# A token-shift expert kernel: the first term of its mix on ScalarE, a second load queue and zero matmuls at the start

## The reference

```python
# x: (8, 1024, 512); 16 experts; w_key (16, 512, 1024); w_value (16, 1024, 512); C = 512 slots per expert
xprev = jnp.concatenate([shift_state[:, None, :], x[:, :-1]], axis=1)
dxprev = xprev - x
xk = x + dxprev * time_maa_k
xr = x + dxprev * time_maa_r
e_idx = token_ids.reshape(N).astype(jnp.int32) * HASH_PRIME % E
...
pos = jnp.take_along_axis(jnp.cumsum(onehot, axis=0), e_idx[:, None], axis=1)[:, 0] - 1
keep = pos < C
...
h = jnp.square(jax.nn.relu(jnp.einsum('ecd,edf->ecf', expert_in, w_key)))
expert_out = jnp.einsum('ecf,efd->ecd', h, w_value)
...
r = jax.nn.sigmoid(jnp.einsum('btd,ed->bte', xr, w_recept))
return r * y            # and x + r * y is the output
```

## Time and profile before

| what | value |
|---|---|
| median of 3 runs | 894.66 us (894.54 to 895.29) |
| span of the profiled execution | 892.5 us |
| TensorE busy | 878.1 us, 98% of the span |
| vector engine busy | 774.1 us, 87% |
| ScalarE busy | 379.8 us, 43% |
| GpSimd busy | 546.4 us, 61% |
| DMA | 186.40 MB, mean 209 GB/s |

### The profile page before, as it was taken

One profiled execution on the slowest core, in us unless ns is written; L12 is line 12 of the kernel. 1 busy time (PEld: TensorE's weight loads), 2 busy tenths in 40 slices (PEclk: granted clock), 3 DMA queues, 4 the chain that ended last, 5 costly groups with the idle time before them and its releaser, 6 DMA issues.

```text
span 892.5 us, 10891 instructions
## 1 busy us (share of the span) xinstructions
PE 878.1 (98%) x3915; PEld 726.6 (81%) x3915; DVE 774.1 (87%) x1060; ACT 379.8 (43%) x582; POOL 546.4 (61%) x485
## 2 busy tenths in 40 slices
PE   6999999999999999999999999999999999999997
PEld 5878888888888888888888888888888888888886
DVE  7999999869898989898989898989898989889862
ACT  4444434555353434443444434343435353535350
POOL 2322215767776767777676777676767677762411
PEclk9999999999999999999999999999999999999999
DMA  9655548865757575858584848484857575754521
GB/s 329 217 176 194 196 142 275 274 218 195 255 176 264 171 270 167 276 169 266 163 278 147 281 147 292 143 286 154 275 167 260 178 253 181 249 192 174 173 87 47
DMA packets 73765, 186.40 MB, mean 209 GB/s; under 512 B 11760, under 2 KB 11760, under 8 KB 73712
## 3 DMA queue, kind: packets, MB, share of 16 engines
q1 hardware_dynamic: 46064, 101.80, 34.9%
q0 software_dynamic: 27648, 83.91, 27.2%
HBM read 152.11 MB, written 33.55 MB: 208 GB/s over the span
## 4 chain that ended last, share of the span: by engine, by line
PE 95%; DVE 2%; issue 1%; DMA 0%; POOL 0%; ACT 0%; SPq 0%; DVEq 0%; POOLq 0%
PE acc L774 32%; PE acc L776 31%; PE acc L775 31%; DVE xr_lo L652 1%; DMA wr_raw<-w_recept_t 0%; DVE mix L643 0%; PE rt_bank L809 0%; DVE mix L646 0%; DVE cum L532 0%; POOL out L359 0%; DVE onehot L526 0%; DVE id_low L524 0%; PE rt_bank L818 0%; DVE totals L536 0%; DVE gate L698 0%
## 5 line engine op out<-in xcount | busy, mean ns | idle before, releaser
L774 PE MATMUL acc<-xk_hi,wk_hi 128*128 128x512 f32 x512 | 199.7, 390 | 0.0
L776 PE MATMUL acc<-xk_hi,wk_lo 128*128 128x512 f32 x512 | 199.6, 390 | 0.0
L775 PE MATMUL acc<-wv_lo,h_hi 128*128 128x512 f32 x512 | 199.5, 390 | 0.0
L774 PE MATMUL acc<-wv_hi,h_hi 128*128 128x512 f32 x512 | 199.5, 390 | 0.0
L776 PE MATMUL acc<-wv_hi,h_lo 128*128 128x512 f32 x512 | 199.4, 390 | 0.0
L775 PE MATMUL acc<-xk_lo,wk_hi 128*128 128x512 f32 x512 | 199.3, 389 | 0.0
L441 ACT ACTIVATE hid<-acc 128x512 f32<-128x512 f32 x128 | 76.6, 599 | 266.1 <-PE acc L776 266.1
L352 POOL DMA_INDIRECT pair_even<-pairs,row_pair x128 | 141.0, 1102 | 65.7 <-issue 38.7
L352 POOL DMA_INDIRECT pair_odd<-pairs,row_pair x128 | 139.7, 1091 | 39.0 <-issue 39.0
L359 POOL DMA_INDIRECT out<-xrow,row_tok x64 | 85.0, 1327 | 111.9 <-DVE xrow L701 102.1
L686 DVE TENSOR_TENSOR hid<-hid 128x512 f32<-128x512 f32 x128 | 88.4, 690 | 51.6 <-ACT hid L441 49.8
(11 more groups left out here) (105 smaller groups left out, 1231.7 us busy)
## 6 DMA issues: line engine op xcount, KB each, us to landing
raw<-w_key SPq DMA_DIRECT2D x64, 512.0 KB, 4.8
raw<-w_value SPq DMA_DIRECT2D x64, 512.0 KB, 4.0
xT<-xs_t SPq DMA_DIRECT2D x64, 256.5 KB, 4.0
gates<-gate SPq DMA_DIRECT2D x64, 256.0 KB, 2.9
pair_even<-pairs,row_pair POOLq DMA_INDIRECT x128, 3.0
pair_odd<-pairs,row_pair POOLq DMA_INDIRECT x128, 3.0
wr_raw<-w_recept_t SPq DMA_DIRECT2D x4, 256.0 KB, 4.6
xrow<-x,row_tok POOLq DMA_INDIRECT x64, 4.8
```

The lines of the kernel that those rows point to most:

```text
L774: pe.matmul(bank[:, :], hi, m_hi, start=first, stop=False)
L775: pe.matmul(bank[:, :], hi, m_lo, start=False, stop=False)
L776: return pe.matmul(bank[:, :], lo, m_hi, start=False, stop=last)
```

## The change

- Loads: `maar` and the first `wr_raw` chunk, as two column halves with a semaphore each, are issued by ScalarE ahead of everything else it does. SyncE loads the first `xT` chunk in two halves, then for k = 1 to 3 `wr_raw` before `xT`. The three first raw weight loads move to the begin of SyncE's step g = 3.
- Mix: the formula becomes x * (1 - maar) + previous * maar. GpSimd makes `keep_r` = 1 - maar. ScalarE writes x * keep_r to the mix slot (`term`), the vector engine adds previous * maar with one instruction (`mix_xr`). The subtractions on the vector engine and on GpSimd are gone, and with them `POOL_DIFF`. The left half of step 0 is mixed in the old way by `mix_left`, which writes `xr_hi` itself.
- Order: ScalarE does term(n + 1) ahead of split_xr(n), and the sigmoids of group g after split 4g + 7 (5 for group 0, 10 for group 1). The vector engine mixes one step ahead of its `xr_lo`.
- TensorE: seven matmuls on zeros into `rt_bank` at the start; steps 0 to 2 run pass by pass, all hi x hi first, each pass with its own wait; step 0 in halves.

```diff
--- before.py
+++ after.py
@@ -74,7 +74,9 @@
...
-    POOL_DIFF = [g * KD + k for g in range(2, 11) for k in (1, 3)]
+    HALF = C // 2
+    WARM = 7
+    SIG_AFTER = [g * KD + min(5 + g, 2 * KD - 1) for g in range(G)]
...
@@ -250,9 +260,14 @@
                 if g >= X_SLOTS:
                     sp.wait_ge(s_mix, KD * (g - X_SLOTS) + k + 1)
                 first = g * C + g // GB
-                sp.dma_start(xT[:, g % X_SLOTS, k, :],
-                             xs_t[k * P:(k + 1) * P, first:first + 1 + C]).then_inc(
-                                 s_x[g % X_SLOTS][k], 16)
+                rows = slice(k * P, (k + 1) * P)
+                if g == 0 and k == 0:
+                    sp.dma_start(xT[:, 0, 0, 0:1 + HALF], xs_t[rows, 0:1 + HALF]).then_inc(s_x_left, 16)
+                    sp.dma_start(xT[:, 0, 0, 1 + HALF:1 + C], xs_t[rows, 1 + HALF:1 + C]).then_inc(
+                        s_x[0][0], 16)
+                else:
+                    sp.dma_start(xT[:, g % X_SLOTS, k, :],
+                                 xs_t[rows, first:first + 1 + C]).then_inc(s_x[g % X_SLOTS][k], 16)
             def store_gates(g):
                 for t in range(ST):
...
-            for k in range(KD):
+            load_group(0, 0)
+            for k in range(1, KD):
+                sp.dma_start(wr_raw[:, k, :], w_recept_t[k * P:(k + 1) * P, :]).then_inc(s_wrec[k], 16)
                 load_group(0, k)
-                if k == 0:
-                    sp.dma_start(maar[:, :], maa_r[:, :]).then_inc(s_maar, 16)
-                sp.dma_start(wr_raw[:, k, :], w_recept_t[k * P:(k + 1) * P, :]).then_inc(s_wrec[k], 16)
             for k in range(KD):
                 load_group(1, k)
             sp.dma_start(id_i, ids.rearrange("b (q j) -> (b q) j", j=J)).then_inc(s_ids, 16)
             sp.dma_start(maak[:, :], maa_k[:, :]).then_inc(s_maak, 16)
-            for n in range(RAW_SLOTS):
-                load_weight(n)
             for k in range(KD):
                 load_group(2, k)
             for g in range(G):
+                if g == 3:
+                    for n in range(RAW_SLOTS):
+                        load_weight(n)
                 if g + X_SLOTS < G:
...
@@ -307,6 +322,8 @@
             pool.affine_select(out=ident[:, :], in_=ident[:, :], compare_op=ALU.not_equal, fill=1.0,
                                base=0, pattern=[[-1, P]], channel_multiplier=1).then_inc(s_ident, 1)
             pool.iota(residue[:, :], [[unhash, E]], base=0, channel_multiplier=0).then_inc(s_table, 1)
+            pool.wait_ge(s_maar, 16)
+            pool.tensor_scalar(keep_r[:, :], maar[:, :], -1.0, 1.0, ALU.mult, ALU.add).then_inc(s_keep, 1)
             pool.memset(segment[:, :, :], 1.0).then_inc(s_zero, 1)
             pool.wait_ge(s_zero, 2)
...
@@ -403,12 +411,25 @@
         @block.scalar
         def _(act):
-            def split_xr(g, k):
-                n = g * KD + k
+            def term(n):
+                g, k = divmod(n, KD)
+                first = HALF if n == 0 else 0
+                act.wait_ge(s_x[g % X_SLOTS][k], 16 * (g // X_SLOTS + 1))
+                if n == 0:
+                    act.wait_ge(s_keep, 1)
+                if n >= MIX_SLOTS:
+                    act.wait_ge(s_rlo, n - MIX_SLOTS + 1)
+                act.activation(mix[:, n % MIX_SLOTS, first:C], xT[:, g % X_SLOTS, k, 1 + first:1 + C],
+                               ACT.Copy, scale=keep_r[:, k:k + 1]).then_inc(s_term, 1)
+            def split_xr(n):
+                g, k = divmod(n, KD)
+                first = HALF if n == 0 else 0
                 act.wait_ge(s_mix, n + 1)
                 if g >= 2:
                     act.wait_ge(s_R, ST * (g - 1))
-                act.copy(xr_hi[:, g % 2, k, :], mix[:, n % MIX_SLOTS, :]).then_inc(s_rhi, 1)
+                act.copy(xr_hi[:, g % 2, k, first:C], mix[:, n % MIX_SLOTS, first:C]).then_inc(s_rhi, 1)
             def sigmoids(g):
                 for t in range(ST):
@@ -444,31 +465,45 @@
                 act.wait_ge(s_sq, n + 1)
                 act.copy(h_hi[:, n % KF, :], hid[:, n % H_SLOTS, :]).then_inc(s_hhi, 1)
-            def split_w_recept(k):
+            def split_w_recept(k, cols=slice(0, D)):
+                act.copy(wr_hi[:, k, cols], wr_raw[:, k, cols]).then_inc(s_wrhi, 1)
+            left, right = slice(0, D // 2), slice(D // 2, D)
+            act.dma_start(maar[:, :], maa_r[:, :]).then_inc(s_maar, 16)
+            act.dma_start(wr_raw[:, 0, left], w_recept_t[0:P, left]).then_inc(s_wrec[0], 16)
+            act.dma_start(wr_raw[:, 0, right], w_recept_t[0:P, right]).then_inc(s_wrec_right, 16)
+            act.wait_ge(s_zeros, 1)
+            act.activation(sigmoid_table[:, :], zeros[:, 0:1], ACT.Sigmoid)
+            act.wait_ge(s_wrec[0], 16)
+            split_w_recept(0, left)
+            act.wait_ge(s_wrec_right, 16)
+            split_w_recept(0, right)
+            term(0)
+            term(1)
+            split_xr(0)
+            for k in range(1, KD):
                 act.wait_ge(s_wrec[k], 16)
-                act.copy(wr_hi[:, k, :], wr_raw[:, k, :]).then_inc(s_wrhi, 1)
...
-            act.activation(sigmoid_table[:, :], ident[:, 0:1], ACT.Sigmoid)
-            for k in range(KD):
                 split_w_recept(k)
-                split_xr(0, k)
...
-            for g in range(G):
-                for k in range(KD):
-                    if g + 1 < G:
-                        split_xr(g + 1, k)
-                    if g * KD + k in FIRST_KEY:
-                        split_weight(FIRST_KEY.index(g * KD + k))
...
-                    if k == min(g, KD - 1):
-                        sigmoids(g)
+                term(k + 1)
+                split_xr(k)
+            for n in range(KD, (G + 1) * KD):
+                r = n - KD
+                if n + 1 < G * KD:
+                    term(n + 1)
+                if n < G * KD:
+                    split_xr(n)
...
+                if n in SIG_AFTER:
+                    sigmoids(SIG_AFTER.index(n))
...
@@ -629,28 +664,38 @@
                                   quarter[:, 0:1], ALU.mult, ALU.add).then_inc(s_rows, 1)
...
-            def mix_xr(g, k):
-                n = g * KD + k
...
-                if n in POOL_DIFF:
-                    dve.wait_ge(s_pool_diff, pool_diffs)
-                else:
-                    if n >= MIX_SLOTS:
-                        dve.wait_ge(s_rlo, n - MIX_SLOTS + 1)
-                    dve.tensor_tensor(slot, xT[:, g % X_SLOTS, k, 0:C], here,
-                                      ALU.subtract).then_inc(s_diff, 1)
-                    dve.wait_ge(s_diff, n + 1 - pool_diffs)
-                dve.scalar_tensor_tensor(slot, slot, maar[:, k:k + 1], here,
-                                         ALU.mult, ALU.add).then_inc(s_mix, 1)
+            def mix_left():
+                slot = mix[:, 0, 0:HALF]
+                before, here = xT[:, 0, 0, 0:HALF], xT[:, 0, 0, 1:1 + HALF]
+                factor = maar[:, 0:1]
+                dve.wait_ge(s_x_left, 16)
+                dve.tensor_tensor(slot, before, here, ALU.subtract).then_inc(s_left, 1)
+                dve.wait_ge(s_left, 1)
+                dve.wait_ge(s_maar, 16)
+                dve.scalar_tensor_tensor(xr_hi[:, 0, 0, 0:HALF], slot, factor, here,
+                                         ALU.mult, ALU.add).then_inc(s_hi_left, 1)
+                dve.scalar_tensor_tensor(slot, slot, factor, here, ALU.mult, ALU.add).then_inc(s_left, 1)
...
+                dve.tensor_tensor(xr_lo[:, 0, 0, 0:HALF], slot, xr_hi[:, 0, 0, 0:HALF].bitcast(F32),
+                                  ALU.subtract).then_inc(s_lo_left, 1)
...
+            def mix_xr(n):
+                g, k = divmod(n, KD)
+                first = HALF if n == 0 else 0
+                slot = mix[:, n % MIX_SLOTS, first:C]
+                dve.wait_ge(s_term, n + 1)
+                dve.scalar_tensor_tensor(slot, xT[:, g % X_SLOTS, k, first:C], maar[:, k:k + 1],
+                                         slot, ALU.mult, ALU.add).then_inc(s_mix, 1)
...
@@ -702,17 +747,18 @@
             route = routing()
-            dve.wait_ge(s_maar, 16)
+            dve.memset(zeros[:, :], 0.0).then_inc(s_zeros, 1)
+            mix_left()
             mixed = 0
             for r in range(-KD, G * KD):
                 n = r + KD
-                while mixed < min(G * KD, n + (1 if n == 0 else min(KD, 2 + max(0, r) // KD))):
-                    mix_xr(*divmod(mixed, KD))
+                while mixed < min(G * KD, n + 2):
+                    mix_xr(mixed)
                     mixed += 1
                 if r < 0:
-                    dve.wait_ge(s_wrhi, n + 1)
+                    dve.wait_ge(s_wrhi, n + 2)
...
@@ -775,6 +821,43 @@
                 pe.matmul(bank[:, :], hi, m_lo, start=False, stop=False)
...
+            def warm():
+                pe.wait_ge(s_zeros, 1)
+                for i in range(WARM):
```

(82 more changed lines are left out.)

15 lines of the change are left out of this document (7 added, 8 removed).

## The result

The changed kernel takes 891.94 us (median of 6 runs, 891.27 to 893.05), the kernel before 894.79 us beside it (6 runs, 894.37 to 895.72): a ratio of 0.9965 with a 95% interval of 0.9955 to 0.9975, 2.85 us less. The forecast was 892.0.

A forecast was written before the change was run, and what follows sets the result against it. TensorE, busy 98% of 892.5 us, was the bound; only its two waits and slow first matmuls could move. Gains of 1.51 (start) and 1.19 us (second wait) took 894.66 to 892.0, range 890.9 to 894.0.

The forecast's parts named there:

- The wait near 46: TensorE's second wait, ahead of matmul 156, from the vector engine's backlog: claimed to vanish, 1.19 us, bounds 0 and 1.19.
- The first real matmul: TensorE's matmul 0, after the first weight's second half lands at 5.3: claimed at about 5.8 and not 7.73.
- The effective start: Where TensorE's line of 0.227 us matmuls, extended back, begins: claimed to move from 9.25 to 7.74, gaining 1.51 us.
- the second `xT` at 7.07: Landing of the second xT chunk, taken as the fourth 256 KB; a landing not near 7.07 would make the prediction wrong.
- rival (b): Start-up loads: two queues fill the DMA engines, second xT lands at 6.4 or sooner; 891.3, at 6.0 890.9; chance 14%.
- The clock: TensorE's start: 2.4 GHz level taken as granted by matmul 8 after seven zero matmuls; bounds 0 and 1.52 us.
- rival (a): TensorE's start: zero matmuls or the gaps leave the clock low, 892.0 + 1.5 = 893.5 us; chance 15%.
- the signs that were to confirm the prediction: TensorE's timeline: seven zero matmuls, matmul 0 near 5.8, a wait ended by xr_hi or lows, matmul 8 near 9.5, none near 45.
- The price of ScalarE's term: ScalarE's x * keep_r in the mix: taken as 0.62 us, bound 1.05, which would put the effective start at 8.17.
- Halves: Half-width casts on ScalarE and subtractions on the vector engine: taken as 0.42 us each, at most the whole.
- Parts at nothing: Moved raw weight loads, GpSimd's keep_r and ScalarE's table load of 1.28 us: claimed to cost no time.
- rival (d): Group boundaries: ScalarE in series with the mix makes TensorE wait for sigmoids; about 898 us; chance 5%.

The follow-up runs named there:

- e3: Kernel before with only the new mix (term on ScalarE, no subtractions) and the old start; step 41's small matmuls start at 124.37 us, against 125.38 before.
- e4: Changed kernel with the old mix (subtractions on vector engine and GpSimd), so the new start alone; step 41's small matmuls start at 124.53 us, against 125.38 before.
- e9: Changed kernel with eleven zero matmuls in place of seven, second trace; 891.24 us, ratio 0.996 to the kernel before.
- e7: Changed kernel with the three raw weight loads back ahead of group 2's xT; step 41's small matmuls start at 124.30 us, against 122.55 in the changed kernel.
- e4b: Second trace of the changed kernel with the old mix; step 41's small matmuls start at 124.70 us, against 125.38 in the kernel before.
- e2: Changed kernel with eleven zero matmuls in place of seven, first trace; step 41's small matmuls start at 122.19 us, against 122.55 in the changed kernel.
- e5: Changed kernel with eleven zero matmuls, split_xr(0) ahead of term(1), no mixing ahead until the fourth step; step 41's small matmuls start at 123.34 us, against 122.55.
- e3b: Second trace of the kernel before with only the new mix; step 41's small matmuls start at 125.44 us, against 125.38 in the kernel before.
- e1: Changed kernel without its zero matmuls, first trace; step 41's small matmuls start at 123.41 us, against 122.55 in the changed kernel.
- e10: Changed kernel without its zero matmuls, second trace; step 41's small matmuls start at 123.38 us, against 122.55 in the changed kernel.
- e6: Changed kernel with maar and both first wr_raw halves issued by SyncE, so one load queue; step 41's small matmuls start at 123.39 us, against 122.55.

## Why the prediction held, step by step

- **The wait near 46: right.** Forecast 1.19 us; e3 shows 1.38 and e4 that the start alone does not remove it. The missing 0.2 lies in how a wait is counted. The profile counts it from the modelled end of the small matmul ahead of it, which starts at 44.70 and is given 0.17 us, while the next matmul would have started 0.03 behind it, as in the changed kernel (second and third line). That is 0.14 us; the slower restart behind the wait is the other 0.05.
```profile
44.70 0.17 PE L796 MATMUL rt_bank<-totals,ones 128*128 128x16 bf16 x1
...
43.24 0.17 PE L879 MATMUL rt_bank<-totals,ones 128*128 128x16 bf16 x1
43.27 0.47 PE L820 MATMUL acc<-wr_hi,xr_hi 128*128 128x512 f32 x1
```
- **The first real matmul: 0.3 us later than forecast.** It came at 6.08 and not 5.8, because the second half of the first weight was there at 5.6 and not at 5.3.
- **The effective start: the size right, by two errors, which is luck.** Forecast 7.74; measured 10.55 - 12 x 0.227 = 7.83, a gain of 1.42 and not 1.51. The first error was the second `xT` at 7.07, one of the prediction's own signs of being wrong. It landed at 6.2, since its issue stands at 2.19 as in the kernel before, where the earlier trace rows gave 2.19 + 4.2 = 6.4; I had ranked it by bytes, on the ground that the engines were 89% busy. They were busy in the earlier trace rows at 183 GB/s, and with work from two queues moved 334 in the same window: a busy share is not a rate. This was the condition of rival (b), whose 891.3 or less did not come with it. The chain of data behind it was 0.65 us ahead of the forecast: `xr_lo` of the right half starts at 8.36 and not 9.01. In e9, where `xT` came at 6.96, it starts at 8.99, as forecast.
- **The clock: its moment right by luck, its part in the sum wrong.** It was taken as up by matmul 8, and it was (9.62, forecast 9.48). The ground given, a burst of zeros as long as the work ahead of the rise before, does not carry it: with the same seven matmuls it rose between 4.4 and 15.5. And I held matmuls 0 to 7 for hidden under the wait for data. They were not: `xr_lo` of the right half was ready at 8.36 + 0.42 = 8.78 (vector engine's row below), and it was the eight slow matmuls from 6.08 that filled the time to 9.62. What the early `xT` gave, the clock took, and no wait of TensorE is left in this stretch. Clock and data chain run side by side and are not added; rival (a)'s 1.5 us assumed the sum. So of the signs that were to confirm the prediction, the wait ended by `xr_hi` or the lows is missing in this trace; it stands in e9's. The slowest run, 893.05, is near rival (a)'s 893.5.
```profile
8.36 0.42 DVE L696 TENSOR_TENSOR xr_lo<-mix,xr_hi 128x256 fp32r<-128x256 f32 x1
```
- **The price of ScalarE's term:** 0.62 was taken with 1.05 as bound; it is 0.72 or 0.73 for a whole width in these traces, over the 0.7 that the prediction named as a sign of being wrong. In the changed kernel's trace, where TensorE has no wait in this stretch, that cost nothing. The Trainium skill (ScalarE: Activation LUTs, "What ACT_TABLE_LOAD costs") states about 93 ns more for a pointer operand; on the 0.62 of the cast that gives 0.71, an estimate with which the trace agrees.
- **Halves:** 0.42 was taken; the cast of 256 columns takes 0.40 and the subtraction 0.42 to 0.43.
- **Parts at nothing:** right for the raw loads (e7), for `keep_r` (GpSimd makes it at 3.21, its first reader is at 5.94) and for the table load (2.22 to 3.50, ahead of the first weight at 4.53).
- **Slower, rival (d):** not seen; at 0.72 a term, ScalarE stays far from the 1.5 at which it would decide. Its working has a slip: 0.5 + 5 x 1.28 + 3.63 is 10.5 and not 10.0, which is 0.3 us over its limit of 10.2 and not 0.2 under it. No wait for a gate came all the same, so this count puts more in series than the engines do.

So the total is right because its larger terms are (the second wait, and a start that clock and data reached together), while two terms inside the start were wrong in opposite directions.

Left open: why the second `xT` landed at 6.2 in one trace and at 6.96 in e9, with the same loads; and whether the slower runs of the changed kernel are those in which the clock came late.

## What to carry to other kernels

When the first instructions of the bottleneck engine are sped up, ask at once whether the engines that feed it keep pace over the next steps: here 1.7 us of a lead of 2.6 (e4), or 0.8 of 1.5 (e4b), went back into waits as long as the feeding engine had one instruction more a step. Take the clock and the data chain of a start-up as two lines side by side and add the later one, not both. Work put there to raise the clock should reach near the first real matmul: seven matmuls with gaps of 1.4 to 4.9 us behind them brought a rise with the burst in one trace of six, eleven with gaps of at most 0.8 us brought it ahead of all traces without zeros in three of three.

## What the runs showed of the hardware

- TensorE rose to the 2.4 GHz level 2.8 to 6.2 us behind the begin of the burst (e2, e4, e5, e9) or of the real matmuls (the others), and 2.0 us differently in two traces of one kernel's start (e3 3.7, e3b 5.7). Single traces of a start-up can't be compared closer than that by their marks.
- Matmuls on zeros in bf16, which leave nothing, count for the clock as real ones do: behind eleven of them the real matmuls of e9 and e5 ran at a pitch of 0.23 us from the first on, and so did e4's behind seven; in e2 the first two were still slow; without any (e1, e10, e3, e3b) at 0.43.
- Loads of 256 KB issued in the first 3.7 us take 3.0 (e6) to 5.3 us (e9) to land, and the same load of one kernel took 4.0 us in the changed kernel and 4.7 in e9.
- A busy share of the 16 DMA engines is not a rate: between 3.50 and 5.00 they were 89% busy at 183 GB/s in the kernel before, 90% at 219 in e6, and full at 334 in the changed kernel.
